# A slot of a scan in another order on VectorE, and a convolution and its token norm as one stage

## The reference, cut to what matters

```python
    x = x + _L1_conv_ref(_gn(x), ...)         # depthwise 3x3, batch norm, relu, prune, 1x1, batch norm, relu, prune
    t = _to_tokens(x)
    t = t + _L2_attn_ref(_ln_t(t), ...)       # _ln_t: each token minus its mean, over its deviation (128 channels)
...
    t = t + _L3_attn_ref(_ln_t(t), ...)       # the scan

    def rosa_scan(x):
        """Per-diagonal recurrence y[r,c] = x[r,c] * (y[r-1,c-1] + 1) on the lower
        triangle of each [T,T] matrix; upper triangle of the output is 0."""
    def rosa_attn_score(x, tau):
        x = x + p                             # p[r,c] = c / (r + 1)
        x = jnp.where(mask, -jnp.inf, x)      # causal
        return jax.nn.softmax(x / tau, axis=-1)
```

## Time and profile before

| what | us |
|---|---|
| median of 3 runs | 3854.08 (3847.75 to 3857.21) |
| the profiled execution, its own time | 3845.83 |
| its span in the profile | 3844.1 |
| TensorE busy (matmuls) | 3294.1, 86% |
| VectorE busy | 3087.6, 80% |
| ScalarE busy | 1888.9, 49% |
| GpSimd busy | 1077.9, 28% |
| from the convolution's first instruction to the norm's last | 955.95 to 1103.64 |
| the state updates of the scan's two groups | 1853.99 to 2621.3 and 2754.3 to 3522.3 |

### The profile page before, as it was taken

How to read it: one execution, slowest core, us unless ns; L and a number is a source line. 1 busy time by engine, 2 the same in 40 slices (tenths; PEclk the granted TensorE clock), 3 DMA queues, 4 the chain that set the end, 5 groups by cost and what they waited for, 6 DMA issues and landing times. The chain is left out here.

```text
span 3844.1 us, 131192 instructions
## 1 busy us (share of the span) xinstructions
PE 3294.1 (86%) x53977; PEld 2075.7 (54%) x53977; DVE 3087.6 (80%) x7677; ACT 1888.9 (49%) x4422; POOL 1077.9 (28%) x1932
## 2 busy tenths in 40 slices
PE   5999999997768849966799999997689999999329
PEld 1323223332357636643577888775377788877214
DVE  7878788883868856668789999997778999997677
ACT  1666566666245524444566655553466655554200
POOL 1000111100003455520455434331165533332000
PEclk7999999999889969975799999997599999999659
DMA  7023333200010122240000000000000000000128
GB/s 151 18 41 57 57 57 57 54 8 10 0 67 27 35 57 77 78 150 18 8 10 13 12 4 9 9 6 5 7 10 10 10 10 10 10 4 6 52 95 301
DMA packets 104351, 155.92 MB, mean 41 GB/s; under 512 B 17060, under 2 KB 65193, under 8 KB 103728
## 3 DMA queue, kind: packets, MB, share of 16 engines
q1 hardware_dynamic: 90064, 121.41, 12.6%
q0 software_dynamic: 12544, 21.93, 2.1%
q10 hardware_dynamic: 1152, 4.19, 0.3%
HBM read 103.21 MB, written 45.30 MB: 39 GB/s over the span
## 5 line engine op out<-in xcount | busy, mean ns | idle before, releaser
L2095 ACT ACTIVATE s_E<-s_Y,s_M 128x9 f32<-128x9 f32 (+38 forms) x2048 | 656.6, 393 | 626.1 <-DVE s_M L2008 624.2
L369 DVE TENSOR_REDUCE half_max<-shared 128x1 f32<-128x512 f32 x1024 | 644.1, 684 | 85.7 <-PE shared L290 83.9
L1909 PE MATMUL g_x<-s_ik,s_iqm 128*32 128x1 f32 (+63 forms) x16384 | 675.2, 280 | 25.8 <-DVE g_o L1991 11.6
L492 ACT ACTIVATE E<-sc 128x1024 f32<-128x1024 f32 x512 | 497.0, 1021 | 276.1 <-PE sc L304 276.0
L2003 DVE SCALAR_TENSOR_TENSOR s_Y<-s_Y,g_x 128x9 f32<-128x9 f32 (+38 forms) x2048 | 578.2, 282 | 46.6 <-PE g_x L1909 1.2
L1921 PE MATMUL g_p<-mats,s_E 128*128 128x128 f32 x3072 | 449.9, 284 | 40.6 <-ACT s_E L2095 36.8
L1909 PEld LDWEIGHTS g_x<-s_ik,s_iqm 128*32 128x32 f32 x16384 | 393.7, 116 | 152.7 <-issue 77.1
L1921 PEld LDWEIGHTS g_p<-mats,s_E 128*128 128x128 f32 x3072 | 340.3, 144 | 107.1 <-ACT s_E L2095 62.6
L290 PE MATMUL shared<-ks,qs 96*128 96x512 bf16 x1024 | 373.6, 402 | 20.4 <-DVE half_max L369 16.7
L2008 DVE TENSOR_REDUCE s_M<-s_Y 128x4 f32<-128x8 f32 (+56 forms) x512 | 351.1, 686 | 0.2
L2019 DVE TENSOR_TENSOR resid<-g_p,s_W 128x512 f32<-128x512 f32 x384 | 263.6, 686 | 61.8 <-PE g_p L1921 58.1
(11 more groups left out here) (358 smaller groups left out, 5054.4 us busy)
## 6 DMA issues: line engine op xcount, KB each, us to landing
e_spread<-d_gate SPq DMA_DIRECT2D x64, 512.0 KB, 6.0
d_parts<-parts SPq DMA_DIRECT2D x8, 1536.0 KB, 5.9
qs<-d_parts SPq DMA_DIRECT2D x96, 128.0 KB, 7.6
ks<-d_parts SPq DMA_DIRECT2D x96, 128.0 KB, 12.4
me_xg<-d_xs SPq DMA_DIRECT2D x144, 65.0 KB, 1.8
mc_yb<-d_ys SPq DMA_DIRECT2D x8, 1024.0 KB, 5.8
resid<-in_x SPq DMA_DIRECT2D x8, 512.0 KB, 8.1
rden<-d_den POOLq DMA_DIRECT2D x16, 256.0 KB
```

Source lines behind the costliest of these rows:

```text
L369: dve.tensor_reduce(half_max[n // SETS % 2][:, idx // 2, idx % 2:idx % 2 + 1], bank("bm", n)[:, :], AX_X, ALU.max).then_inc(max_done, 1)
L492: act.activation(E[:, G % 2, h, :], sc[n % 2][:, :], ACT.Exp, scale=0.25).then_inc(exp_done, 1)
L1909: mm = pe.matmul(x_ps[u % 3][32 * b:32 * (b + 1), rho % 2, 0:n + 1], iqm[n // WINDOW % 2][:, b, x0:x0 + D, :], s.ik[:, b, rho, 0:n + 1], s ...
L2095: act.activation(E[:, m % 2, rho, 0:m + 1], Y[:, D * (m % YR) + rho, 1:2 + m], ACT.Exp, bias=M[:, D - 1 + D * m + rho:D + D * m + rho]).th ...
```

## The change

In `scan_rows` the maximum of the preceding quad becomes the first VectorE instruction of a slot, ahead of all four state updates. Nothing else moves there; each instruction keeps its waits.

`layer1_conv` becomes `conv_and_norm`, one block that also holds the token norm n2; the block of its own and its barrier go. VectorE's iteration b is now `taps(b)`, `norm(b-2)`, `finish(b-1)`, `prune(b)`, `moments(b-1)`, where `moments` are the statistics and `norm` is reciprocal, shift and four scaled tiles, with the bodies that they had. ScalarE and TensorE get the norm's steps between their own. The PSUM has room for this because the taps' sum, the product and the transposed input have one buffer each now (two, two and three before); the waits for a free buffer are tightened to match. `t.add_xn`, which only allocates the norm's output, moves ahead.

```diff
-def layer1_conv(nc, t):
+def conv_and_norm(nc, t):
...
-        taps_ps = [ctx.enter_context(nc.psum_tensor(f"c_taps{i}", [P, 2 * HALF], F32)) for i in range(2)]
-        ps = [ctx.enter_context(nc.psum_tensor(f"c_ps{i}", [P, 2 * HALF], F32)) for i in range(2)]
...
+        taps_ps = ctx.enter_context(nc.psum_tensor("c_taps", [P, 2 * HALF], F32))
+        ps = ctx.enter_context(nc.psum_tensor("c_ps", [P, 2 * HALF], F32))
+        turned_in = ctx.enter_context(nc.psum_tensor("c_in", [P, NT, P], F32))
+        turned_out = ctx.enter_context(nc.psum_tensor("c_out", [P, T], F32))
...
-                for b in range(B):
-                    taps(b)
+                def moments(b):
+                    dve.wait_ge(turned, b + 1)
                     if b:
+                        dve.wait_ge(stat, 2 * b)
+                    for j in range(NT):
+                        bn = dve.bn_stats(stats[:, j, :], turned_in[:, j, :])
+                    bn.then_inc(stat, 1)
+                    dve.wait_ge(stat, 2 * b + 1)
+                    if b >= 2:
+                        dve.wait_ge(deviated, b - 1)
+                        dve.wait_ge(moved, b - 1)
+                    for j in range(NT):
+                        bn = dve.bn_aggr(mv[b % 2][:, j, :], stats[:, j, :])
+                    bn.then_inc(stat, 1)
+
+                def norm(b):
+                    i = b % 2
+                    dve.wait_ge(deviated, b + 1)
+                    if b >= 2:
+                        dve.wait_ge(scaled, b - 1)
+                        dve.wait_ge(back, b - 1)
+                    dve.reciprocal(rstd[i][:, :], std[i][:, :]).then_inc(recip, 1)
+                    dve.wait_ge(recip, b + 1)
+                    dve.scalar_tensor_tensor(shift[i][:, :], mv[i][:, :, 0], -1.0, rstd[i][:, :], ALU.mult, ALU.mult
+                                             ).then_inc(moved, 1)
+                    for j in range(DVE_TILES):
+                        ts = dve.tensor_scalar(xt[i][:, j, :], turned_in[:, j, :], mv[i][:, j, 0:1],
+                                               rstd[i][:, j:j + 1], ALU.subtract, ALU.mult)
+                    ts.then_inc(normed, 1)
+
+                for b in range(B + 2):
+                    if b < B:
+                        taps(b)
+                    if b >= 2:
+                        norm(b - 2)
+                    if 1 <= b <= B:
                         finish(b - 1)
-                    prune(b)
-                finish(B - 1)
+                    if b < B:
+                        prune(b)
+                    if 1 <= b <= B:
+                        moments(b - 1)
 
             @block.scalar
...
-                for b in range(B):
-                    if b:
+                def deviation(b):
+                    i = b % 2
+                    act.wait_ge(stat, 2 * b + 2)
+                    if b >= 2:
+                        act.wait_ge(recip, b - 1)
+                    act.activation(std[i][:, :], mv[i][:, :, 1], ACT.Sqrt, bias=t.vec("eps5")).then_inc(deviated, 1)
+
...
+                for b in range(B + 2):
+                    if 1 <= b <= B:
                         activate(b - 1)
-                    hide(b)
+                    if b < B:
+                        hide(b)
+                    if b >= 2:
+                        scale(b - 2)
                     if b + 2 < B:
                         put(b + 2)
-                activate(B - 1)
+                    if b >= 2:
+                        store(b - 2)
+                    if 1 <= b <= B:
+                        deviation(b - 1)
...
                 def taps(b):
                     pe.wait_ge(padded, b + 1)
-                    if b >= 2:
-                        pe.wait_ge(tap, TAPS * (b - 2) + 1)
+                    if b:
+                        pe.wait_ge(tap, TAPS * (b - 1) + 1)
                     for h in range(2):
...
                 def main(b):
                     pe.wait_ge(kept, b + 1)
-                    if b >= 2:
-                        pe.wait_ge(second_done, 2 * b - 2)
+                    if b:
+                        pe.wait_ge(second_done, 2 * b)
                     for h in range(2):
...
+                def turn_in(b):
+                    pe.wait_ge(added, b + 1)
+                    if b:
+                        pe.wait_ge(normed, b)
+                        pe.wait_ge(scaled, b)
+                    for j in range(NT):
+                        c0 = b * T + j * P
+                        tr = pe.transpose(turned_in[:, j, :], t.resid[:, c0:c0 + P], t.mat("ident"))
+                    tr.then_inc(turned, 1)
+
+                def turn_out(b):
...
+                    pe.wait_ge(scaled, b + 1)
+                    if b:
+                        pe.wait_ge(stored, b)
+                    for j in range(NT):
+                        tr = pe.transpose(turned_out[:, j * P:(j + 1) * P], xt[b % 2][:, j, :], t.mat("ident"))
+                    tr.then_inc(back, 1)
...
                 pe.wait_ge(diag_done, 1)
                 taps(0)
-                for b in range(B):
-                    if b:
+                for b in range(B + 3):
+                    if b >= 3:
+                        turn_out(b - 3)
+                    if 2 <= b < B + 2:
+                        turn_in(b - 2)
+                    if 1 <= b <= B:
                         main(b - 1)
                     if b + 1 < B:
                         taps(b + 1)
-                main(B - 1)
...
@@ -2051,11 +2147,10 @@
 
                 dve.wait_ge(zeroed, ZEROED)
                 for n in range(SLOTS):
-                    if n < QUADS:
-                        recur(n, 0)
                     if 0 <= n - 1 < QUADS:
                         maximum(n - 1)
                     if n < QUADS:
+                        recur(n, 0)
                         recur(n, 1)
                     if 0 <= n - 2 < QUADS:
                         weigh(n - 2, 0)
...
-        layer1_conv(nc, t)
         t.add_xn(nc, ctx)
-        token_norm(nc, t, "n2", "eps5")
+        conv_and_norm(nc, t)
```

More of the change, by code:

```diff
@@ L670, in taps @@
                                 dve.wait_ge(hidden_done, b - 1)
-                            before = taps_ps[b % 2][:, :].rearrange("p (y x) -> p y x", y=SIDE)
+                            before = taps_ps[:, :].rearrange("p (y x) -> p y x", y=SIDE)
                         else:
@@ L729, in activate @@
                             act.wait_ge(added, b - 1)
-                        act.activation(second[b % 2][:, h * HALF:(h + 1) * HALF], ps[b % 2][:, h * HALF:(h + 1) * HALF],
+                        act.activation(second[b % 2][:, h * HALF:(h + 1) * HALF], ps[:, h * HALF:(h + 1) * HALF],
                                        ACT.Relu, bias=off[:, 1:2], scale=inv[:, 1:2]).then_inc(second_done, 1)
@@ L738, in _, with scale, store @@
                 act.wait_ge(folded, 9)
-                for b in range(B):
-                    if b:
+                def deviation(b):
[4 more added lines that the diff above has]
+                    act.activation(std[i][:, :], mv[i][:, :, 1], ACT.Sqrt, bias=t.vec("eps5")).then_inc(deviated, 1)
+                def scale(b):
+                    i = b % 2
+                    act.wait_ge(moved, b + 1)
+                    if b >= 2:
+                        act.wait_ge(back, b - 1)
+                    for j in range(DVE_TILES, NT):
+                        sc = act.activation(xt[i][:, j, :], turned_in[:, j, :], ACT.Identity,
+                                            bias=shift[i][:, j:j + 1], scale=rstd[i][:, j:j + 1])
+                    sc.then_inc(scaled, 1)
+                def store(b):
+                    act.wait_ge(back, b + 1)
+                    act.activation(t.xn[:, b * T:(b + 1) * T], turned_out[:, :], ACT.Copy).then_inc(stored, 1)
+                for b in range(B + 2):
+                    if 1 <= b <= B:
                         activate(b - 1)
-                    hide(b)
+                    if b < B:
+                        hide(b)
+                    if b >= 2:
+                        scale(b - 2)
                     if b + 2 < B:
                         put(b + 2)
-                activate(B - 1)
+                    if b >= 2:
+                        store(b - 2)
+                    if 1 <= b <= B:
+                        deviation(b - 1)
             @block.tensor
```

15 lines of the change are left out of this document (13 added, 2 removed).

## The result

| what | before | after |
|---|---|---|
| median of 8 runs each on one chip | 3855.64 (3847.75 to 3864.7) | 3846.53 (3836.75 to 3851.87) |
| ratio, 95% interval | | 0.9975, 0.9964 to 0.9986 |
| the profiled execution, its own time | 3845.83 | 3851.87 |
| its span | 3844.1 | 3850.1 |
| VectorE busy | 3087.6 | 3125.3 |

The change makes the kernel 9.1 us faster by the medians (5.4 to 13.9 by the interval). The forecast was 3846.6. By the bound of the prediction, 0.3%, that counts as the same. With eight runs a side the interval is narrower than that bound, and it excludes a ratio of 1, so the gain is small but real.

What follows compares the result with a forecast made beforehand. VectorE bounds convolution and norm, engines take turns in the early scan, TensorE bounds the late scan. 3845.8 - 9.5 + 2 = 3838.3 for the profiled execution, 8.25 under the median, so forecast 3846.6; range 3831 to 3866, its own 3840 to 3852.

Steps and rivals of the forecast that it cites:

- Bound and method: Whole kernel by stage: VectorE bounds convolution and norm, three engines take turns in the early scan, TensorE fills the late scan.
- Joining, -9.5: Convolution and norm: of 18.3 us that are not VectorE's work, 8.8 stay as ramps and handovers; gain 9.5 us.
- The cover of the transposes: Joined stage: 1.63 us from `finish` to the end of `prune` hide 1.04 us of transposes and two handovers.
- the third rival: Joined stage: TensorE at the lower clock throughout, 22.2 us a batch against 14.58, 61 us more, 3907; chance 0.05.
- Edges on VectorE, +38 us of its time: Scan: maximum first adds 0.03 us in 256 slots and 0.12 in 256, 38 us of VectorE's time.
- Scan, late: 0: Slots 128 to 255: 9.6 us added a group go into VectorE's 13 us of waits for full TensorE; 0.
- Scan, early: +2: Slots 0 to 127: chunks with both VectorE waits cost nothing; half the added time stands in the last quarter, +2 us.
- One of the prediction's own signs of being wrong: Early scan: chunks that change by more than 0.3 us would show the forecast wrong.
- the sixth slot's wait: Early scan: VectorE's wait ending a chain from the third slot's maximum, which moves 0.14 us earlier and as much later.
- The first rival: Early scan: the exponentials were the limit; 30 TensorE waits a group shrink by 0.23 us, gaining 14, 3830; chance 0.17.
- The second (3853): Joined stage: VectorE waits about 0.8 us a batch for the single turned buffer, giving back 6.4 us; chance 0.17.
- The fourth (3883): Scan: VectorE paces it and its added edges are absorbed nowhere, so 38 us replace the 2; chance 0.11.

Runs made afterwards that it cites:

- the second profile of before: The kernel before, profiled again with no edit: 3853.41 us; convolution with its norm 147.05 us, state updates of the two groups 773.90 and 772.42 us.
- experiment 1: The changed kernel with the old order in the scan, so only the joined stage: 3841.72 us, ratio to before 0.9959.
- experiment 3: The changed kernel with the maximum first only in slots with nothing between the last update and the next: state updates 771.87 and 772.25 us.
- experiment 5: The changed kernel with the maximum behind the first two state updates of a slot: state updates 783.17 and 782.27 us.
- experiment 8: The changed kernel with the old scan order and two extra waits of `recur(n, 0)` moved one VectorE instruction earlier: 3837.42 us, ratio to before 0.9941.
- experiment 10: The joined stage with the old scan order, run once more with no new edit: 3845.31 us, ratio to before 0.9968.
- experiment 6: The changed kernel with `moments(b-1)` ahead of `prune(b)` on VectorE: a joined stage of 158.04 us.
- experiment 4: The changed kernel with the maximum first only in the third slot of each chunk: state updates 772.25 and 772.67 us.
- experiment 2: The kernel before with the maximum first in the scan, convolution and norm still apart: 3860.07 us against 3854.39, ratio 1.0012.

## Why the prediction was right

**Bound and method.** The reading that the early scan has slack on several engines and that the late one belongs to TensorE held. Slots 160 to 223 take 116.53 and 123.52 us in every kernel of the table, to 0.04, whatever VectorE does there.

**Joining, -9.5.** From the first tap to the end of the last store it was to be 125.4 us. It is 1103.95 + 1.02 - 979.60 = 125.4. The pieces came out near the forecast: 1.4 for the relu (1.3); 2.6 for the late turns (2.1 + 0.4); 0.7 for the two roots (0.8); and 3.4 for the transposes back and the store, from 1101.6 on (3.1). The 0.7 for a late last product did not come: it took 2.01 us, at the full clock's price, and nothing waited for its relu. Handovers of about 0.7 in all take its place, where the prediction had rounded up by 0.4. A batch takes 14.58 (14.6), TensorE has a granted clock of 1.00 in the middle, and the statistics never wait there. The stage as a whole gains 147.69 - 138.80 = 8.9, because the first tap comes 13.43 us after the stage's start and not 12.80. Against the second profile of before it gains less, and in experiments 1, 3, 5, 8 and 10, where it is the same stage, more. The mean of the two profiles of before is 147.7 for the stage start to start, and of the two of after 139.6: 8.1, with kernels of the same stage 137.9 to 139.6. The term was 9.5 and the runs show 8 to 10.

**The cover of the transposes.** The sentence that 1.63 us of pruning cover 1.04 us of transposes, and that the price is the third rival's if the cover goes, was tested in experiment 6. The cover is real. The price without it was 18.4 us, with the later product in it: more than the 9 expected of the uncovered transposes alone and less than the rival's 61, since the lower clock held for a part of each batch only.

The Trainium skill, "Perfetto Trace Analysis", section Identifying Performance Opportunities, says that a gap that repeats can mean too little PSUM. With one buffer each, no wait for the transposes repeats on VectorE in the changed kernel (2 waits, 2.6 us). With the same buffers and another order there is one in each of eight batches (18.4 us). The buffers are the same in both kernels, so the gap came from the order.

**Edges on VectorE, +38 us of its time.** The three edge prices are borne out by the timeline above, and that of 0.13 by experiment 8, which turned it into 0.04 by moving waits and nothing else. VectorE's busy time grew from 3087.6 to 3125.3, by 37.7, but that this is nearly 38 is in part chance. Busy time counts the overlap of 0.08 that each slot lost, 512 x 0.08 = 41, and not the gaps, which by the same prices shrank by 256 x 0.05 and grew by 256 x 0.04.

The Trainium skill, "VectorE: DVE Perf Modes", section The DRAIN you can't avoid, says of eight copies in a row that a semaphore after each costs nothing extra. In this case's short updates it does cost something: an update starts 0.08 us ahead of its predecessor's end if what it waits for is long done, 0.04 after that end if it waits for that predecessor, and 0.13 after it if that wait stands in an instruction of its own.

**Scan, late: 0.** Right from slot 144 on, the last 32 slots with it (129.09 us in both orders). It was mis-sized for slots 128 to 159, +0.4 and +0.5 in the two groups, with +0.60 in the first chunk of eight. The late part was taken as one window with TensorE full, and in these 32 slots it is busy 104.48 of 105.99 us before. VectorE's waits in the late part fell to 6.8 and not to 3. The forecast took all of the added 9.6 as paid from them, and 5.2 was seen there; since the chunks keep their length, the rest went into waits too short for that view.

**Scan, early: +2.** The step was that chunks with both waits absorb their added edges and that half of the rest stands in the last 32 early slots. For those it gave 1.2 a group, and 1.15 and 1.45 came. The sum was mis-sized by what it had put at nothing: +0.4 in slots 64 to 95, beside the 0.4 to 0.5 of slots 128 to 159. One of the prediction's own signs of being wrong, early chunks that change by more than 0.3 us, did appear: the three chunks of slots 104 to 127 grew by 0.32 to 0.53. The length of slots 0 to 63 differs by over 2 us between profiles of one kernel and tells nothing. Over all kernels, the state updates of both groups took 1547.9 to 1548.8 us in the new order (four profiles) and 1544.0 to 1546.3 in the old (six, with experiments 3 and 4, which took its time). The term is about +3 and not +2. Experiment 3 puts it in the slots behind `least`, `rescale` and `divide`, to which the prediction had given four fifths of the added time.

**One step was wrong in its detail.** The prediction moved the sixth slot's wait "by nothing", since the third slot's maximum comes 0.14 earlier and is pushed back by as much. The outcome holds (experiment 4 changes nothing), but the reason does not. With the third slot's maximum freed of what pushes it back, the limit passes to the fourth slot's. The first rival had the same error in another form: it paid for each of 30 waits as if nothing else were due at the same time.

**The sum.** The terms were -9.5 + 2 = -7.5, taken from the median of before, 3854.1. The stages show -8.1 + 3.1 = -5.0 between the means of the two profiles of each kernel, the times -9.1 (5.4 to 13.9). That the forecast met the median to 0.1 us is luck. The median of before was 3855.6 in eight runs and not 3854.1, and the change gained 1.6 us more than forecast; the two cancel. Whether anything beside the two stages was gained stays open: their 5 to 7 us lie at the low end of the interval or just under it, and a first attention that varies by 10 us between executions is enough to hide the rest.

**The rivals.** The first (3830) falls with experiments 2 and 4. The second (3853) falls with the two waits of the statistics, and its premise, a turned buffer that comes late, is what experiment 6 makes. The third (3907) did not occur. The fourth (3883) falls with experiment 2; experiment 5 shows that this scan can be lengthened by 21 us through the order of three instructions, so the rival's mechanism exists, with another order; in its last 32 slots VectorE has no wait left and paces.

## What to carry to other kernels

Where two stages are joined that keep the same engine busy, count the time in which that engine does not work, subtract the ramps that the joined stage will still have, and check for each single buffer what work of the bounding engine covers its turnaround. In a loop that several engines pace in turns, put independent work between two instructions of which one needs the other, and keep the wait for the instruction just ahead apart from other waits, which can run earlier. VectorE's busy time counts neither gaps nor what overlaps, so price an order from a timeline. When a change is worth less than the spread of an untouched stage, compare the stages, not the spans.

## What the runs showed of the hardware that was not expected

An instruction with two further waits, for which the trace shows no time waited, started 0.09 us later than one that waits for its predecessor alone (0.13 against 0.04). The traces show an instruction of the sequencer of 0.05 us in between, which holds the wait for the predecessor. With the two waits one instruction earlier it ran during other work, and the 0.09 was gone, although the instruction that carries them now follows its own predecessor by 0.04 as before.

The product behind a pause of 4.06 us on TensorE ran 3.78 us and not 1.98. The granted clock was 1.00 up to 1015 us, 0.59 in the mean of 1015 to 1017 and 0.50 from 1017 to 1021. The stage grew by 18.4 us where the uncovered transposes alone were expected to cost some 9.

A stretch in which TensorE was busy from end to end kept its 129.09 us while VectorE's waits for it shrank from 2.4 us to 0.4, and grew by 0.87 when none were left.

The first attention, the same instructions in every kernel here, took from 928.8 to about 942 us, and the difference lies in how long ScalarE waited for TensorE.
